# Moving the LayerNorm's normalisation from VectorE to ScalarE, and re-placing six small jobs, in a fused attention and mixture-of-experts kernel

## The chip, the cores and the metric

The kernel is one launch on one core of a Trainium2 chip. The metric is the device time in microseconds (us). The kernel before took 1573.0 us, the median of 3 runs (1572.06 to 1573.33).

## The reference, cut to what matters

The input is `x`, 64 sequences of 128 rows by 256, with a context of 64 x 128 x 192. Two layers follow one another.

```
x = x + attention(layernorm(x), context)   # 16 heads of 64; q = n @ Wq, k,v = ctx @ Wkv, softmax, @ Wproj + bproj
x = x + experts(layernorm(x))              # 8 experts 256x256, silu, top 2 of a softmax gate, then combine_w
layernorm(x) = (x - mean) / sqrt(var + 1e-5)
```

Everything is float32. The kernel keeps a product's precision by splitting each operand into a high part (`fp32r`) and a low part (what the high part leaves), and adding three products.

## The kernel before, in words

**Pairs and slots.** Two sequences make a pair; there are 32 pairs. The attention of a pair has 8 slots (`u` 0 to 7), one for each pair of heads. A slot is a row of instructions on each engine that `for s, i, u in slots()` writes out: slot `s`, pair `i`, number `u`. The slots before slot 0 (`i == -1`) are the start, those after pair 31 the tail. Each engine runs its own instructions strictly in the order in which they stand; semaphores hold an engine back until another has got far enough.

**What a slot holds.** TensorE (PE): `turn_probs` of the head pair before (4 transposes), `queries_keys` three head pairs ahead (11 matmuls), `scores` of the next head pair (6), then the slot's general jobs ("mid"), then `attend` (6) and `project` (6), and in late slots the `expert` and `combine` products. ScalarE (ACT): `exps`, `pT`, `attended`, `qk` and then the high parts of the general jobs. VectorE (DVE): `inverse` (the sums of the exponentials and their reciprocals), `pT`, `qk`, `row_max`, then the low parts of the general jobs. GpSimd (POOL): `split_attended`, `normalise_probs`, `scatter` and `gather` by indirect DMA, `rsqrt`, `split_ctx_lo`, `add_bias` in slot 0. So there is one chain for every slot: `turn_probs` (PE), `pT` and `attended` (ACT), `split_attended` and `normalise_probs` (POOL), and `turn_probs` of the next slot (PE).

**General jobs.** `ATTENTION_JOBS` says in which slot PE makes the values of the next pair (`value`, four jobs of 5 matmuls of 512 columns), the transposes of the two normalised inputs (`turn_x`, `turn_x1`), the gate and the ranks. They share three PSUM banks in turn.

**Experts.** Tokens are scattered to a sorted table, and 147 blocks of 128 sorted rows run through their experts, at one block a slot. The blocks are listed when a chunk of pairs is routed; the chunks end at pairs 8, 16, 22, 26 and 28. In the first slots after such a pair DVE runs `count_blocks`, `list_blocks` and `list_outputs`. Blocks fill the slots from pair 9 slot 6 to pair 14 slot 4, from 17.6 to 22.4, from 23.6 to 27.4, and from 27.6 to 32.3. The other slots, here called light, hold attention alone (and now and then a combine). The last four pairs' experts are computed densely, in the tail.

**LayerNorm.** For each of the two norms: DVE `norm_stats` and `norm_merge` (mean and variance, two of each), POOL `rsqrt` (`var_eps`, then `rstd` by a power), DVE `normalise` (two `tensor_scalar`, line 1006). For the next pair's `x` the statistics stand in slot 5 (of the pair two earlier), `rsqrt` in slot 6 and `normalise` in slot 1; for `x1` of the pair before they stand in slot 2, 2 and 3. `turn_x` is in slot 3, `turn_x1` in slot 4. `normalise(j, n)` waits for POOL's `rstd_done`, PE's `turn_x` and `turn_x1` wait for `xn_done` and `xn2_done`.

**The start.** SyncE (SP) loads the weights. ACT makes their high parts (`weight_hi`), DVE the low parts of the first six, POOL those of the rest of the keys (6 and 7) and of the projection. PE's `queries_keys(0, 2)`, in the last slot before slot 0, waits for all of these but the projection's. In slots 1 to 8 DVE prepares the expert weights (`expert_minus_last`) and POOL splits them. In pair 1 slot 0 SP writes zero rows into the sorted table (line 538).

Of the kernel before, what the change touches and what calls it, by code (L numbers as in the profile page):

```python
# [5 lines left out]
P = 128  # L6
# [37 lines left out]
    6: [("value", 1, 1)],  # L44
    7: [("rank", 0, -1)],
# [94 lines left out]
def xattn_moe_kernel(nc, x, ctxT, wq, wkv, wkv_rest, wproj, bproj, gateT, expertT, expert_b, combineT, out):  # L140
# [20 lines left out]
    with ExitStack() as stack:  # L161
# [93 lines left out]
        rstd = [sb(f"rstd{n}", [P, 2]) for n in (1, 2)]  # L255
        neg_max = [sb(f"neg_max{b}", [P, 4]) for b in range(2)]
# [83 lines left out]
        rstd_done = [sem(f"rstd_done{n}") for n in (1, 2)]  # L340

# [52 lines left out]
        FOR_FIRST, FOR_VALUES, BY_VECTOR, PROJECTION, EXPERTS_FROM, COMBINE_SPLIT = 3, 5, 6, 8, 9, len(SPLIT) - 1  # L394
        KEYS_BY_POOL = PROJECTION - BY_VECTOR
        PROJ_BY_POOL = KEYS_BY_POOL + 1
# [3 lines left out]
        def _(sp):  # L400
# [29 lines left out]
            def load_weights(n):  # L430

                if n >= EXPERTS_FROM:
                    sp.wait_ge(w_lo_dve, BY_VECTOR)
                if n > EXPERTS_FROM:
                    sp.wait_ge(w_lo_pool, KEYS_BY_POOL)
                of, to = WEIGHTS[n]
                sp.dma_start(to, of).then_inc(w_in[n], 16)
# [66 lines left out]
            for s, i, u in slots():  # L504
# [31 lines left out]
                if i == 1 and u == 0:  # L536
# [32 lines left out]
        def _(pe):  # L569
# [9 lines left out]
            def queries_keys(j, p):  # L579
# [7 lines left out]
                if j == 0 and p == 2:  # L587
                    pe.wait_ge(w_hi, PROJECTION)
                    pe.wait_ge(w_lo_dve, BY_VECTOR)
                    pe.wait_ge(w_lo_pool, KEYS_BY_POOL)  # L590
# [116 lines left out]
            def combine(m, bank):  # L707
                pe.wait_ge(drained["turn_mixed"], m + 1)
                if m == 0:
                    pe.wait_ge(w_lo_pool, COMBINE_SPLIT - BY_VECTOR + 1)  # L710
# [56 lines left out]
            pe.wait_ge(const_b, 2)  # L767
            for s, i, u in slots():
# [29 lines left out]
        def _(act):  # L798
# [6 lines left out]
            def weight_hi(n):  # L805
# [9 lines left out]
                act.activation(hi, raw, ACT.Copy, scale=QSCALE if n in (0, FOR_VALUES) else 1.0).then_inc(w_hi, 1)  # L815

# [93 lines left out]
            for s, i, u in slots():  # L910
# [46 lines left out]
        def _(dve):  # L957
# [6 lines left out]
            def weight_lo(n):  # L964
# [5 lines left out]
                else:  # L970
                    rows = HALF if n in (2, 4) else P
# [17 lines left out]
            def stats_ready(j, n):  # L989
                dve.wait_ge(bn_done[n], 2 * j + 2)  # L990
                wait(dve, (xn_done, xn2_done)[n], j)
# [10 lines left out]

            def normalise(j, n, src, to, done, width=C):
                dve.wait_ge(rstd_done[n], j + 1)
                for t in range(2):
                    last = dve.tensor_scalar(to[:, t, 0:width], src[:, t, 0:width], mv[n][:, t, 0:1], rstd[n][:, t:t + 1],
                                             ALU.subtract, ALU.mult)
                last.then_inc(done, 1)
# [161 lines left out]
            def count_blocks():  # L1170
# [5 lines left out]
                link(dve.tensor_tensor_scan(rows_to[:, :], rows_new[:, :], zeros[:, :], 0.0, ALU.add, ALU.add))  # L1176
                link(dve.tensor_tensor(rows_from[:, :], rows_to[:, :], rows_new[:, :], ALU.subtract))
# [60 lines left out]
            for s, i, u in slots():  # L1238
# [42 lines left out]
                if u == (1 if i > 0 else 2) and nxt:  # L1281
                    normalise(i + 1, 0, x_raw, x_raw, xn_done)
                if u == 3 and before:
                    wait(dve, made["turn_x1"], i - 1)
                    wait(dve, scattered[(i - 1) % 2], 64 * min((i - 1) // 2, (SPARSE + i % 2) // 2))
                    if i - 1 < 2:
                        dve.wait_ge(const_c, 3)
# [35 lines left out]
        def _(pool):  # L1323
# [14 lines left out]
            def rsqrt(j, n):  # L1338
                pool.wait_ge(mv_done[n], 2 * j + 2)
                wait(pool, rstd_done[n], j)  # L1340
# [139 lines left out]
```

## Time and profile before

| what | value |
|---|---|
| median of 3 runs | 1573.0 us |
| the profiled execution | 1573.3 us |
| its span, first to last instruction | 1571.6 us |
| mean granted TensorE clock, share of full speed | 0.994 |
| busy: PE, DVE, ACT, POOL | 95%, 82%, 67%, 59% |

The profiled execution's time is 1.7 us more than its span and 0.3 us over the median. Busy shares are averages over the span: a PE that is called busy may still run matmuls at a wider spacing than it can. L12 is line 12 of the kernel, `a<-b,c` what an instruction writes and reads, `x4` the number of instructions that one row merges. A wait is put down to what released it.

### The profile page before, as it was taken

How to read it: one execution, taken by the hardware profiler on the slowest of the kernel's cores; microseconds unless marked ns; L12 is line 12 of the kernel's file. 1: busy time of each engine (PE TensorE's matmuls, PEld its weight loads, DVE VectorE, ACT ScalarE, POOL GpSimd, SP SyncE). 2: the span in 40 equal slices, each digit the busy share in tenths (PEclk: the TensorE clock that was granted, in tenths of full speed). 3: DMA queues.
4: the chain of work that ended last, by engine and by line, in shares of the span. 5: the costliest groups of instructions: out<-in, count | busy, mean ns of one | idle time of the engine just before them, and what ended most of it. 6: DMA issues, size and time to landing. Idle time of an engine off the chain costs nothing.

```text
span 1571.6 us, 38337 instructions
## 1 busy us (share of the span) xinstructions
PE 1499.9 (95%) x11648; PEld 1435.2 (91%) x11648; DVE 1292.8 (82%) x3153; ACT 1057.0 (67%) x2891; POOL 923.7 (59%) x1215
## 2 busy tenths in 40 slices
PE   5999999999999999999999999999999999999796
PEld 4889999999899999999999999989999999999675
DVE  6988888888888888888888888888888888877566
ACT  4766776766667766676667677767777676767432
POOL 5756666666555655577666555576666466655510
PEclk9999999999999999999999999999999999999999
DMA  8543333333577777455677777568888777877822
GB/s 241 179 132 97 95 94 94 96 95 98 169 223 229 224 219 215 110 135 146 196 236 235 208 225 220 161 172 241 244 241 239 232 223 236 266 215 222 279 61 81
DMA packets 180474, 287.77 MB, mean 183 GB/s; under 512 B 23600, under 2 KB 115248, under 8 KB 180016
## 3 DMA queue, kind: packets, MB, share of 16 engines
q1 hardware_dynamic: 169520, 255.94, 57.2%
q0 software_dynamic: 10752, 29.37, 5.7%
q8 instruction: 97, 1.59, 0.4%
q14 instruction: 105, 0.86, 0.2%
HBM read 156.51 MB, written 61.60 MB: 139 GB/s over the span
## 4 chain that ended last, share of the span: by engine, by line
PE 75%; DVE 12%; issue 6%; ACT 4%; POOL 3%; DMA 1%; SPq 0%; ACTq 0%; DVEq 0%; POOLq 0%
PE gen_ps L572 20%; PE qk_ps L572 17%; PE o_ps L572 9%; PE proj_ps L572 9%; PE s_ps L572 9%; PE pT_ps L617 6%; PE gen_ps L695 2%; DVE neg_max L1019 1%; DVE sums L1026 1%; PE gen_ps L662 1%; PE gen_ps L670 1%; DVE pT_s_lo L961 1%; DMA k_s<-qk_s 1%; ACT v_s_hi L802 1%; ACT stage L802 1%
## 5 line engine op out<-in xcount | busy, mean ns | idle before, releaser
L1357 POOL CAST o_s_hi<-stage 128x256 fp32r<-128x256 f32 x256 | 102.0, 398 | 413.7 <-ACT stage L802 409.8
L828 ACT ACTIVATE stage<-s_ps,neg_max 128x128 f32<-128x128 f32 x1024 | 292.1, 371 | 73.9 <-DVE neg_max L1019 69.8
L1348 POOL TENSOR_TENSOR stage<-stage,inv_sums 128x512 f32<-128x512 f32 x256 | 265.9, 1039 | 10.2 <-DVE inv_sums L1028 10.1
L802 ACT CAST pT_s_hi<-pT_ps 128x512 fp32r<-128x512 f32 x256 | 150.6, 588 | 129.6 <-PE pT_ps L617 119.9
L572 PE MATMUL s_ps<-k_s,qk_s 128*128 128x256 f32 x1536 | 226.7, 284 | 3.6 <-DMA k_s<-qk_s 3.3
L1026 DVE TENSOR_REDUCE sums<-stage 128x4 f32<-128x512 f32 x256 | 172.7, 675 | 45.3 <-ACT stage L828 32.4
L961 DVE TENSOR_TENSOR qk_s<-qk_ps,qk_s 128x512 fp32r<-128x512 f32 x256 | 176.3, 689 | 39.2 <-ACT qk_s L802 34.4
L572 PEld LDWEIGHTS s_ps<-k_s,qk_s 128*128 128x128 f32 x1536 | 201.7, 189 | 4.4 <-DMA k_s<-qk_s 3.9
L1359 POOL TENSOR_TENSOR o_s_lo<-stage,o_s_hi 128x256 fp32r<-128x256 f32 x256 | 188.2, 735 | 20.9
L961 DVE TENSOR_TENSOR pT_s_lo<-pT_ps,pT_s_hi 128x512 fp32r<-128x512 f32 x256 | 171.9, 672 | 30.4 <-ACT pT_s_hi L802 24.2
L802 ACT CAST v_s_hi<-gen_ps 128x512 fp32r<-128x512 f32 x129 | 75.8, 587 | 178.0 <-PE gen_ps L572 176.1
L802 ACT COPY stage<-o_ps 64x256 f32<-64x256 f32 x512 | 188.0, 367 | 3.1
L572 PE MATMUL qk_ps<-xT_hi,wq_s_hi 128*128 128x256 f32 x512 | 165.6, 323 | 11.7 <-DVE cT_hi L1013 4.8
L1019 DVE TENSOR_REDUCE neg_max<-s_ps 128x4 f32<-128x512 f32 x256 | 174.4, 681 | 0.9 <-PE s_ps L572 0.9
L572 PE MATMUL o_ps<-pT_s_hi,v_s_hi 128*128 128x256 f32 x512 | 155.6, 304 | 16.5 <-DVE pT_s_lo L961 14.3
L802 ACT CAST qk_s<-qk_ps 128x512 fp32r<-128x512 f32 x256 | 149.7, 585 | 29.5 <-PE qk_ps L572 18.3
L617 PE MATMUL pT_ps<-ident,stage 128*128 128x128 f32 x1024 | 154.8, 273 | 1.4 <-POOL stage L1348 1.0
L572 PE MATMUL proj_ps<-wproj_s_hi,o_s_hi 128*128 128x256 f32 x512 | 146.6, 286 | 3.2 <-POOL o_s_lo L1359 2.8
L572 PE MATMUL qk_ps<-xT_hi,wq_s_lo 128*128 128x256 f32 x512 | 145.1, 283 | 0.0
L572 PE MATMUL o_ps<-pT_s_hi,v_s_lo 128*128 128x256 f32 x512 | 144.9, 283 | 0.0
L572 PE MATMUL o_ps<-pT_s_lo,v_s_hi 128*128 128x256 f32 x512 | 144.4, 282 | 0.0
L572 PE MATMUL qk_ps<-xT_lo,wq_s_hi 128*128 128x256 f32 x512 | 144.3, 282 | 0.0
(347 smaller groups left out, 4655.4 us busy)
## 6 DMA issues: line engine op xcount, KB each, us to landing
w_block<-expert_table SPq DMA_DIRECT2D x147, 512.0 KB
k_s<-qk_s SPq DMA_DIRECT2D x512, 128.0 KB
stage<-sorted_x SPq DMA_DIRECT2D x147, 128.0 KB
sorted_y<-stage SPq DMA_DIRECT2D x147, 128.0 KB
x_raw<-in_x SPq DMA_DIRECT2D x32, 256.0 KB
c_raw<-in_ctxT SPq DMA_DIRECT2D x32, 256.0 KB
stage<-in_x SPq DMA_DIRECT2D x32, 256.0 KB, 3.5
x_kept<-x SPq DMA_DIRECT2D x32, 256.0 KB
```

Of the source, the lines that this page charges most:

```text
L572: mm = pe.matmul(out_ap, l, r, start=start and n == 0, stop=stop and n == len(terms) - 1, skip_group_check=skip)
L617: mm = pe.transpose(pT_ps[:, k * P:(k + 1) * P], probs[p % 2][:, k, :], ident[:, :])
L662: mm = pe.matmul(bank[:, a * N2 + t * P:a * N2 + (t + 1) * P], src[:, 2 * t + k, a * P:(a + 1) * P], ident[:, :], is_transpose=True, start ...
L695: mm = pe.transpose(bank[:, a * P:(a + 1) * P], x_block[n % RING][:, a * P:(a + 1) * P], ident[:, :])
L802: last = act.copy(to, of)
L828: last = act.activation(probs[p % 2][:, k, :], s_ps[:, k * P:(k + 1) * P], ACT.Exp, bias=neg_max[p % 2][:, k:k + 1])
L961: last = dve.tensor_tensor(lo, of, hi.bitcast(F32), ALU.subtract)
L1019: dve.tensor_reduce(neg_max[p % 2][:, :], s_ps[:, :].rearrange("p (k n) -> p k n", k=4), AX_X, ALU.max, negate=True).then_inc(max_done, 1)
L1026: dve.tensor_reduce(sums[p % 2][:, :], probs[p % 2][:, :, :], AX_X, ALU.add).then_inc(sums_done, 1)
L1348: pool.tensor_tensor(probs[b][:, :, :], probs[b][:, :, :], inv_sums[b][:, :].unsqueeze(2).broadcast_to([P, 4, P]), ALU.mult).then_inc(prob ...
L1357: pool.tensor_copy(hi[:, :, :], o_full).then_inc(o_hi, 1)
L1359: pool.tensor_tensor(lo[:, :, :], o_full, hi[:, :, :].bitcast(F32), ALU.subtract).then_inc(o_lo, 1)
```

## The change

The diff, cut to its core. Left out are the new buffers and semaphores (`minus_rstd`, `minus_mean`, `minus_one`, `minus_done`, `shift_done`), a memset of `minus_one`, and the counts of `w_lo_dve` and `w_lo_pool` that follow from who makes which low part.

```diff
-    6: [("value", 1, 1)],
-    7: [("rank", 0, -1)],
+    7: [("rank", 0, -1), ("value", 1, 1)],
...
+        BY_POOL, LAST_KEYS, PROJECTION = 6, 7, 8
+        BY_VECTOR, PROJ_BY_POOL = 7, 2
...  SP, the zero rows
-                if i == 1 and u == 0:
+                if i == 4 and u == 0:
...  PE, before the slots, after const_b
+            for n in range(16):
+                pe.transpose(gen_ps[BANKS - 1][:, 0:P], ident[:, :], ident[:, :])
...  ACT
+            def normalise(j, n, src, to, done, width=C):
+                act.wait_ge(shift_done[n], j + 1)
+                for t in range(2):
+                    last = act.activation(to[:, t, 0:width], src[:, t, 0:width], ACT.Identity,
+                                          bias=minus_mean[n][:, t:t + 1], scale=rstd[n][:, t:t + 1])
+                last.then_inc(done, 1)
...  ACT, in the slots, after general(s, "mid")
+                if u == 2 and nxt:
+                    normalise(i + 1, 0, x_raw, x_raw, xn_done)
+                if u == 3 and before:
+                    wait(act, made["turn_x1"], i - 1)
+                    wait(act, scattered[(i - 1) % 2], 64 * min((i - 1) // 2, (SPARSE + i % 2) // 2))
...
+                    normalise(i - 1, 1, x1, xn2[(i - 1) % 2], xn2_done, C - 1)
...  DVE
-                    rows = HALF if n in (2, 4) else P
+                    rows = HALF if n in (2, 4, LAST_KEYS) else P
...
-            def normalise(j, n, src, to, done, width=C):
-                dve.wait_ge(rstd_done[n], j + 1)
...
+            def chunk_rows():
                 link(dve.tensor_tensor(rows_from[:, :], rows_to[:, :], rows_new[:, :], ALU.subtract))
                 link(dve.tensor_tensor(choices[:, 0, :], begun[:, :], rows_from[:, :], ALU.subtract))
...
-                if s in (-SLOTS, 0):
+                if u == 0 and nxt:
                     x_stats(i + 1)
-                if u == 5 and i >= 0 and exists(i + 2):
-                    x_stats(i + 2)
...
-                if u == (1 if i > 0 else 2) and nxt:
-                    normalise(i + 1, 0, x_raw, x_raw, xn_done)
-                if u == 3 and before:
...
-                    normalise(i - 1, 1, x1, xn2[(i - 1) % 2], xn2_done, C - 1)
...
                     if u == 0:
                         count_blocks()
                     if u == 1:
+                        chunk_rows()
+                    if u == 3:
                         list_blocks(plan.ends.index(i - 1))
...
+                if i == -1 and u == 6:
+                    weight_lo(LAST_KEYS)
...  POOL, in rsqrt, after rstd
+                pool.wait_ge(rstd_done[n], j + 1)
+                pool.tensor_tensor(minus_rstd[n][:, :], rstd[n][:, :], minus_one[:, :], ALU.mult).then_inc(minus_done[n], 1)
+                pool.wait_ge(minus_done[n], j + 1)
+                pool.tensor_tensor(minus_mean[n][:, :], mv[n][:, :, 0], minus_rstd[n][:, :], ALU.mult).then_inc(shift_done[n], 1)
...
-                if s in (-SLOTS + 1, 1):
+                if u == 1 and nxt:
                     rsqrt(i + 1, 0)
-                if u == 6 and i >= 0 and exists(i + 2):
-                    rsqrt(i + 2, 0)
...
-                    for n in range(BY_VECTOR, PROJECTION):
-                        weight_lo(n)
+                    weight_lo(BY_POOL)
```

So `x` is normalised as `rstd * x + minus_mean`, where `minus_mean` is the mean times minus `rstd`; `count_blocks` keeps its first five operations.

## Rows read from the trace of the kernel before

**Rows 1.** The page, part 1: busy us (share of the span) x instructions.

```profile
PE 1499.9 (95%) x11648; PEld 1435.2 (91%) x11648; DVE 1292.8 (82%) x3153; ACT 1057.0 (67%) x2891; POOL 923.7 (59%) x1215
```

**Rows 2.** Busy us (instructions) by stretch, clock, DMA share, GB/s.

```profile
100.00:200.00 100.00, 98.42 (x768) 94.25 (x768) 81.01 (x208) 69.72 (x193) 62.55 (x85) 1.00 0.36 89
500.00:600.00 100.00, 100.00 (x812) 97.95 (x811) 85.54 (x212) 69.92 (x199) 53.16 (x72) 1.00 0.78 224
```

**Rows 3.** Timeline of the start: start us, us, engine, line, [idle before <-releaser].

```profile
6.97 1.14 DVE L1006 TENSOR_SCALAR x_raw<-x_raw,mv,rstd 128x256 f32<-128x256 f32 x2 [1.11 <-POOL rstd L1343]
11.35 0.55 PE L572 MATMUL qk_ps<-xT_hi,wq_s_hi 128*128 128x256 f32 x1 [2.00 <-DVE xT_lo L961]
16.82 0.41 PE L572 MATMUL qk_ps<-xT_lo,wq_s_hi 128*128 128x256 f32 x1
17.19 0.28 PE L572 MATMUL qk_ps<-cT_hi,wkv_s_hi 128*128 128x256 f32 x1
18.21 1.76 DVE L968 SCALAR_TENSOR_TENSOR wq_s_lo<-stage,wq_s_hi 128x1536 fp32r<-128x1536 f32 x1 [0.70 <-ACT wq_s_hi L815]
19.00 2.65 POOL L1330 TENSOR_TENSOR wkv_s_lo<-stage,wkv_s_hi 128x768 fp32r<-128x768 f32 x1 [11.36 <-ACT wkv_s_hi L815]
21.60 1.80 POOL L1330 TENSOR_TENSOR wkvr_s_lo<-stage,wkvr_s_hi 128x768 fp32r<-128x768 f32 x1
23.66 0.36 PE L572 MATMUL qk_ps<-xT_hi,wq_s_hi 128*128 128x256 f32 x1 [4.54 <-POOL wkvr_s_lo L1330]
```

**Rows 4.** Timeline of pair 1, slots 0 to 2.

```profile
76.39 2.38 SPq L420 DMA_DIRECT2D k_s<-qk_s  x2
82.11 0.97 PE L572 MATMUL s_ps<-k_s,qk_s 128*128 128x256 f32 x6 [1.99 <-DMA k_s<-qk_s]
```

**Rows 5.** Timeline of pair 0, slots 2 and 3, and of slot 7.

```profile
42.16 1.73 DVE L1006 TENSOR_SCALAR x_raw<-x_raw,mv,rstd 128x256 f32<-128x256 f32 x2
46.28 0.38 PE L572 MATMUL o_ps<-pT_s_hi,v_s_hi 128*128 128x256 f32 x1 [1.06 <-DVE pT_s_lo L961]
...
66.85 0.39 PE L572 MATMUL o_ps<-pT_s_hi,v_s_hi 128*128 128x256 f32 x1 [0.71 <-DVE pT_s_lo L961]
```

**Rows 6.** Timeline of pair 5, a light pair: slots 3 and 4.

```profile
243.10 1.15 ACT L828 ACTIVATE stage<-s_ps,neg_max 128x128 f32<-128x128 f32 x4
243.80 0.60 PE L617 MATMUL pT_ps<-ident,stage 128*128 128x128 f32 x4
244.97 0.19 POOL L1341 TENSOR_TENSOR var_eps<-mv,eps 128x2 f32<-128x2 f32 x1 [0.85 <-DVE mv L995]
247.09 1.04 POOL L1348 TENSOR_TENSOR stage<-stage,inv_sums 128x512 f32<-128x512 f32 x1
247.74 1.14 ACT L828 ACTIVATE stage<-s_ps,neg_max 128x128 f32<-128x128 f32 x4 [0.20 <-DVE neg_max L1019]
248.18 0.66 PE L617 MATMUL pT_ps<-ident,stage 128*128 128x128 f32 x4
252.54 0.60 PE L617 MATMUL pT_ps<-ident,stage 128*128 128x128 f32 x4
```

**Rows 7.** Groups of instructions: busy us, mean ns | idle before.

```profile
L896 ACT ACTIVATE stage<-stage,top_w 128x256 f32<-128x256 f32 x112 | 47.7, 501 | 0.0
```

**Rows 8.** One line's instructions: duration ns min/median/max, first and last start.

```profile
L1103 DVE SCALAR_TENSOR_TENSOR top_w<-gate_exp,gate_inv x32: 161/164/1609, 115.6 to 1534.4; 128x4 f32<-128x4 f32 x32
L987 DVE BATCH_NORM_STATS2 stats<-x_raw x64: 407/414/421, 4.8 to 1352.3; 128x6 f32<-128x256 f32 x64
```

**Rows 9.** Timeline of slot 0: pair 5, then pair 9 with its block count.

```profile
234.48 0.69 DVE L1026 TENSOR_REDUCE sums<-stage 128x4 f32<-128x512 f32 x1 [0.89 <-ACT stage L828]
234.85 1.31 POOL L1366 TENSOR_TENSOR stage<-stage,bias_row 128x512 f32<-128x512 f32 x1
...
391.38 2.14 DVE L1175 TENSOR_TENSOR rows_new<-rounded,begun 128x9 f32<-128x9 f32 x1
392.17 1.31 POOL L1366 TENSOR_TENSOR stage<-stage,bias_row 128x512 f32<-128x512 f32 x1
```

More of the change, by code:

```diff
@@ L255, in xattn_moe_kernel @@
         rstd = [sb(f"rstd{n}", [P, 2]) for n in (1, 2)]
+        minus_rstd = [sb(f"minus_rstd{n}", [P, 2]) for n in (1, 2)]
+        minus_mean = [sb(f"minus_mean{n}", [P, 2]) for n in (1, 2)]
+        minus_one = sb("minus_one", [P, 2])
         neg_max = [sb(f"neg_max{b}", [P, 4]) for b in range(2)]
@@ L340, in xattn_moe_kernel @@
         rstd_done = [sem(f"rstd_done{n}") for n in (1, 2)]
+        minus_done = [sem(f"minus_done{n}") for n in (1, 2)]
+        shift_done = [sem(f"shift_done{n}") for n in (1, 2)]
         dense_tanh, dense_added, dense_w_done = (sem(n) for n in ("dense_tanh", "dense_added", "dense_w_done"))
@@ L392, in xattn_moe_kernel @@
         SPLIT.append((stage[:, 2, 0:2 * C], *[w[:, :, :].rearrange("p a n -> p (a n)") for w in wcomb_s]))
-        FOR_FIRST, FOR_VALUES, BY_VECTOR, PROJECTION, EXPERTS_FROM, COMBINE_SPLIT = 3, 5, 6, 8, 9, len(SPLIT) - 1
-        KEYS_BY_POOL = PROJECTION - BY_VECTOR
-        PROJ_BY_POOL = KEYS_BY_POOL + 1
+        FOR_FIRST, FOR_VALUES, EXPERTS_FROM, COMBINE_SPLIT = 3, 5, 9, len(SPLIT) - 1
+        BY_POOL, LAST_KEYS, PROJECTION = 6, 7, 8
+        BY_VECTOR, PROJ_BY_POOL = 7, 2
         QSCALE = float(HALF) ** -0.5
@@ L434, in load_weights @@
                 if n > EXPERTS_FROM:
-                    sp.wait_ge(w_lo_pool, KEYS_BY_POOL)
+                    sp.wait_ge(w_lo_pool, 1)
                 of, to = WEIGHTS[n]
@@ L589, in queries_keys @@
                     pe.wait_ge(w_lo_dve, BY_VECTOR)
-                    pe.wait_ge(w_lo_pool, KEYS_BY_POOL)
+                    pe.wait_ge(w_lo_pool, 1)
                 wait(pe, qk_lo, j * HEAD_PAIRS + p)
@@ L709, in combine @@
                 if m == 0:
-                    pe.wait_ge(w_lo_pool, COMBINE_SPLIT - BY_VECTOR + 1)
+                    pe.wait_ge(w_lo_pool, PROJ_BY_POOL + E + 1)
                 for t in range(2):
@@ L938, in _ @@
                 general(s, "mid")
+                if u == 2 and nxt:
[3 more added lines that the diff above has]
+                    wait(act, scattered[(i - 1) % 2], 64 * min((i - 1) // 2, (SPARSE + i % 2) // 2))
+                    if i - 1 < 2:
+                        act.wait_ge(const_c, 3)
+                    normalise(i - 1, 1, x1, xn2[(i - 1) % 2], xn2_done, C - 1)
                 if s in plan.mix and plan.pair_of[plan.mix[s]] < SPARSE:
@@ L990, in stats_ready @@
                 dve.wait_ge(bn_done[n], 2 * j + 2)
-                wait(dve, (xn_done, xn2_done)[n], j)
+                wait(dve, shift_done[n], j)
             def norm_merge(n):
@@ L1001, in x_stats @@
                 norm_merge(0)
-            def normalise(j, n, src, to, done, width=C):
-                dve.wait_ge(rstd_done[n], j + 1)
[L1005 to L1008, printed above, removed]
             def rest_lo(j):
@@ L1280, in _ @@
                     norm_merge(1)
-                if u == (1 if i > 0 else 2) and nxt:
-                    normalise(i + 1, 0, x_raw, x_raw, xn_done)
-                if u == 3 and before:
[L1284 to L1287, printed above, removed]
-                    normalise(i - 1, 1, x1, xn2[(i - 1) % 2], xn2_done, C - 1)
                 if u == 4 and nxt:
@@ L1339, in rsqrt @@
                 pool.wait_ge(mv_done[n], 2 * j + 2)
-                wait(pool, rstd_done[n], j)
+                wait(pool, (xn_done, xn2_done)[n], j)
                 pool.tensor_tensor(var_eps[n][:, :], mv[n][:, :, 1], eps[:, :], ALU.add).then_inc(eps_done[n], 1)
@@ L1400, in _ @@
             pool.memset(eps[:, :], EPS)
+            pool.memset(minus_one[:, :], -1.0)
             pool.memset(minus_half[:, :], -0.5).then_inc(zeroed, 2)
```

## The prediction

> **What bounds the kernel.** I read the page first: PE is busy for 1499.9 of 1571.6 us [rows 1], so at most 72 us are idle, and no job leaves PE but for the order. Then the windows: where expert blocks run, PE is busy for 100.00 of 100 us with 812 matmuls; in light stretches it runs 768 and DVE only 81 [rows 2]. So between expert blocks nothing can be gained, little can be lost, and the change is decided in the start, in pairs 0 and 1 and in the light slots. The timelines of these places came next, with one question at each wait of PE: who is late.
>
> In the start PE waits until 11.35 for the first low part, and then from its last value product (started at about 18.7) to 23.66 for the low part of the last keys, which POOL makes in 2.65 and 1.80 us one after the other [rows 3]. In pair 1 it waits 1.99 us for the spread keys [rows 4], in pair 0 1.06 us for DVE, which had normalised x for 1.73 us just before, and 0.71 us at the end of pair 0, where DVE has no idle time [rows 5]. In light pairs the reader is to look at the distance between the `turn_probs` of two slots: 243.80, 248.18, 252.54, that is 4.38 and 4.36 us [rows 6], while PE's own work there is some 3.9 us. `turn_probs` at 248.18 starts when POOL's `normalise_probs` (247.09, 1.04 us) ends. The chain of a slot (PE's transposes, ACT's `pT` and `attended`, POOL's split and multiply) sets the pace there, and DVE's normalisation at slot 3 isn't in it.
>
> **Part by part.** The price of ACT's normalisation: the trace has no Identity with two pointer operands; the nearest row is ACT's scaled copy of the same 128x256, 47.7 us for 112, so 0.43 us each, 0.85 us for two [rows 7]. From below the 64-row copies of `attended` would give 0.74 for two; from above the 0.50 us of one alone gives 1.0. I take 0.85. POOL's two added operations on 128x2 are like `var_eps`, 0.19 us each [rows 6], and with their waits 0.5 us a norm.
>
> *The start.* POOL's addition (0.5) and the change of engine make the normalised x late by 0.2 us only, since two normalisations took 1.14 us on DVE [rows 3]. But on ACT it stands before the high parts of the context and the first weights, which were made while DVE worked: they slip by 0.85 us, and the first product from 11.35 to 12.2. All to the last high part slips by as much. Then DVE makes the last part in half the rows beside POOL. POOL ends part 6 at 19.00 + 0.85 + 2.65 = 22.5; DVE's part 7 is half of POOL's rows, under 1 us on DVE, after its 1.76 us part at 18.21 + 0.85 and the keys of slot -2, so at 22.5 too. `queries_keys(0, 2)` starts at 22.6 for 23.66: -1.05. The value job that filled the wait (5 products, 1.2 us) now stands after the first scores; PE has time there, but ACT makes its high part before the first exponentials: +0.7. Together -0.4. Between -2 (ACT's queue hidden) and +1 (nothing of the split gained).
>
> The 16 early transposes end before x is ready and cost nothing. Their possible gain: products started every 0.21 us at 16.82 and every 0.12 us after 17.19 (durations 0.41 and 0.28) [rows 3]; were the clock up at 12.2, about 2.1 us of the 24 products before POOL's part would go. No row shows transposes alone raising the clock: four ran at 8.26 and the clock rose 8.8 us later. I take 0. The Trainium skill, "TensorE: Matmul & The Clock Gate", Part 4, says that transposes do not count as busy for the clock gate; by it the gain is 0 as well, by the row alone it stays open.
>
> *Pairs 0 and 1.* The write of zero rows leaves the stretch in which keys of pair 1 landed 3.3 us after their issue ended; in pair 4 the same keys have some 6 us: -2.0, the whole wait [rows 4]. DVE is rid of 1.73 us in pair 0 slot 2, but the exponentials follow ACT's 0.85 us there: -0.7 of the 1.06. Statistics leave slot 5 of pair 0: -0.7 of the late wait [rows 5], given back by half when they stand in slot 0 of pair 1 before DVE's expert rows: net -0.3. POOL's longer `rsqrt` before the combine weights: +0.5. Light slots 3 and 4 of pair 1 (below): +0.8. Sum -1.7, between -4 and +1.
>
> *Light pairs.* Slot 2: exponentials started at 243.10 directly after the value's high part; now 0.85 us later. `pT` and `attended` follow by 0.5 us later than before (0.24 to 0.3 us were idle). POOL's `rsqrt` at 244.97 gets 0.5 us longer and stands before the same split, so the two delays coincide: `normalise_probs` ends at 248.6 for 248.13, +0.5. Slot 3: ACT runs exponentials, `pT`, `attended`, keys, context, x and now x1: 4.9 us, in a slot of 4.4. The exponentials of 247.74 (0.20 us idle before) come 1.3 later, `attended` about 0.7 to 0.9 later, and `turn_probs` at 252.54 by 0.9 in sum [rows 6]. Slot 5 holds the gate and a value job; it is PE's own and gives nothing back.
>
> Slot 0 adds 0.2: the statistics, 0.41 us each and never longer, now stand before DVE's weights of the gate, an operation of 0.16 to 1.61 us [rows 8]. The long ones are those that meet POOL's add of the bias. At 391.38 another small DVE operation with two inputs ran 2.14 us and ended when POOL's 1.31 us add had [rows 9]. In pair 5 it would now begin at 234.35 and end with the add, at 236.2, for sums that started at 234.48: late by 1.6, of which 1.4 are slack. The Trainium skill, "Advanced Engine Details and Errata", GPSIMD Details, states that POOL shares an interface with VectorE's instructions of two SBUF inputs; the trace agrees (2.14 us), and by the rule the 0.2 stands.
>
> Slots 6 and 7: PE waited 0.3 us in slot 7 for DVE; with the value job there it doesn't, but slot 6 without it becomes light and is set by the chain, 4.3 us: -0.1. And -0.05 at the gate's slot. Per light pair 0.9 + 0.2 - 0.15 = 0.95; the terms overlap in ACT's queue, so I take 0.8. Light in slots 3 and 4 are pairs 2 to 9, 15 and 23 (16 and 17 have a combine in slot 3 that covers it): 10 x 0.8 = +8. From below -0.3 a pair (the removed wait alone, the rest hidden), from above 1.3.
>
> *Chunk ends.* Five times `count_blocks` meets the bias add (2.14 us of wait in one [rows 9]). The statistics before it fill that time, and two operations of 0.2 us leave: -0.4 each, -2.0. `list_blocks` in slot 3 meets other POOL work: +0.2 each, +1.0. Sum -1.0, from -5 to +4. SP needs the list at slot 4, after the last scatter of slot 3 anyway.
>
> *Blocks and tail.* With 1.7 us more PE work a slot, ACT's 0.85 fits: 0, at most +0.3 for each of 16 pairs. Tail: one norm, 0 (within 1).
>
> Sum on the profiled 1573.3: -0.4 - 1.7 + 8 - 1.0 = +4.9, 1578.2. I set 1577.5, since of the slack at each link I have counted only what shows as idle time. The median shown is 0.3 lower.
>
> **Rivals.** (a) ACT's additions hide in light slots: the exponentials have a whole slot until their `turn_probs`, ACT is busy 70 of 100 us [rows 2], and if POOL's queue regains 0.5 us in each slot, only the removed waits remain. Then 1573.3 - 0.4 - 1.7 - 1 - 0.1 x 10 - 0.8 (pair 1) = 1568.4, faster. It decides from a light-slot loss below 0.3 us a pair. Against it: idle of 0.20 us only before the exponentials of slot 3 [rows 6]. (b) The transposes raise the clock: 2.1 us off the forecast, 1575.4; with (a), 1566. (c) The loss reaches the block slots too, 16 x 0.3 = 5 more: 1582.5; against it the 100% of PE there.
>
> **Chances.** Forecast 0.45, (a) 0.27, (b) with the forecast's slots 0.15, (c) 0.13. A change under 0.2% (3.1 us) can't be told from none. Slower (above 1576.1): 0.38 of the forecast, 0.06 of (b), (c): 0.57, less some for a sum that is all small terms: 0.5. Same: 0.24. Faster: 0.26. Range 1567 to 1584; the forecast's own is 1574.5 to 1580.5.
>
> **What would show it.** Right: in pair 5 the `turn_probs` of slots 3, 4 and 5 lie 4.9 and 4.7 us apart where they were 4.4; a light pair takes 40.1 us instead of 39.3; no wait for keys in pair 1; first keys of head pair 2 at 22.6; the gate weights' median duration at 1.6 us in light pairs. Wrong: light slots of 4.4 us as before, or a granted clock already up at the first product.

## The result, and the profile after

The kernel after takes 1586.8 us (median of six, 1585.5 to 1588.3) where the kernel before took 1574.2 on the same chip: a ratio of 1.0075, 95% interval 1.0062 to 1.0088, so some 12 us slower. (One of the six executions of the kernel before took 8273 us; with it left out, the median is 1573.3.) The same kernel measured again beside other kernels, as after_again, gave 1.0101 (1.0075 to 1.0126). I had forecast 1577.5, and 1584 as the upper end: the direction is right, the size nearly three times too small.

The profiled execution took 1585.64 us with a span of 1583.9, against 1573.3 and 1571.6. Part 1 of its page answers to [rows 1]:

```profile
PE 1519.9 (96%) x11664; PEld 1441.8 (91%) x11664; DVE 1254.6 (79%) x3026; ACT 1112.8 (70%) x3019; POOL 949.3 (60%) x1343
```

DVE lost 38 us of work, ACT took on 56 and POOL 26. The windows answer to [rows 2]; the third is the stretch from the last scores to the end:

```profile
100.00:200.00 100.00, 98.69 (x748) 91.66 (x748) 80.79 (x195) 71.26 (x197) 62.19 (x90) 1.00 0.37 95
500.00:600.00 100.00, 100.00 (x815) 98.19 (x814) 83.52 (x201) 76.59 (x215) 58.73 (x87) 1.00 0.77 226
1461.60:1583.90 122.30, 93.25 (x499) 79.09 (x497) 76.03 (x171) 46.62 (x106) 29.58 (x37) 0.91 0.42 142
```

PE has 748 matmuls in 100 us of light slots where it had 768, and as many as before (815 for 812) where expert blocks run. The loss is in the light slots. The same last stretch of the kernel before:

```profile
1451.80:1571.60 119.80, 90.32 (x499) 76.31 (x497) 76.39 (x173) 45.61 (x104) 29.14 (x35) 0.94 0.43 143
```

It holds the same 499 matmuls in 2.5 us less, at a granted clock of 0.94 for 0.91. So in this profile the last scores came 9.8 us later than before, and the other 2.5 us are clock in the tail. That split varies from one execution to another: in after_again, a second profile of the same kernel with the same span, the last scores came 13.8 us later and the tail took 118.2 us at 0.94.

The start, answering to [rows 3], and then the keys of pair 1 [rows 4] (`SPq` is SyncE's DMA queue):

```profile
7.54 1.09 ACT L828 ACTIVATE x_raw<-x_raw,minus_mean,rstd 128x256 f32<-128x256 f32 x2 [1.95 <-POOL minus_mean L1360]
12.43 0.55 PE L576 MATMUL qk_ps<-xT_hi,wq_s_hi 128*128 128x256 f32 x1 [2.62 <-DVE cT_hi L1029]
19.64 2.65 POOL L1343 TENSOR_TENSOR wkv_s_lo<-stage,wkv_s_hi 128x768 fp32r<-128x768 f32 x1 [9.70 <-ACT wkv_s_hi L822]
21.42 1.69 DVE L995 TENSOR_TENSOR wkvr_s_lo<-stage,wkvr_s_hi 64x768 fp32r<-64x768 f32 x1
23.21 0.55 PE L576 MATMUL qk_ps<-xT_hi,wq_s_hi 128*128 128x256 f32 x1 [5.08 <-DVE wkvr_s_lo L995]
...
76.24 1.20 SPq L424 DMA_DIRECT2D k_s<-qk_s  x2
80.76 0.88 PE L576 MATMUL s_ps<-k_s,qk_s 128*128 128x256 f32 x6
```

The keys of head pair 2 come at 23.21 for 23.66, and in pair 1 PE doesn't wait for spread keys any more. VectorE's low part in half the rows takes 1.69 us: it ends 0.82 us after POOL's part 6 (`wkv_s_lo`), beside which it started (in start_only it takes 1.09 us and again ends 0.82 us after POOL's). Slots 3 to 5 of pair 5, the light pair of [rows 6]:

```profile
246.00 1.09 ACT L828 ACTIVATE x_raw<-x_raw,minus_mean,rstd 128x256 f32<-128x256 f32 x2
246.70 0.60 PE L621 MATMUL pT_ps<-ident,stage 128*128 128x128 f32 x4
247.00 1.12 ACT L843 ACTIVATE stage<-s_ps,neg_max 128x128 f32<-128x128 f32 x4
249.20 0.20 POOL L1360 TENSOR_TENSOR minus_mean<-mv,minus_rstd 128x2 f32<-128x2 f32 x1
250.52 1.03 POOL L1365 TENSOR_TENSOR stage<-stage,inv_sums 128x512 f32<-128x512 f32 x1
250.73 1.10 ACT L828 ACTIVATE xn<-x,minus_mean,rstd 128x255 f32<-128x255 f32 x2
251.60 0.66 PE L621 MATMUL pT_ps<-ident,stage 128*128 128x128 f32 x4
251.72 1.13 ACT L843 ACTIVATE stage<-s_ps,neg_max 128x128 f32<-128x128 f32 x4
256.28 0.66 PE L621 MATMUL pT_ps<-ident,stage 128*128 128x128 f32 x4
```

ACT's normalisation stands directly ahead of the exponentials in both slots. The `turn_probs` lie 4.90 and 4.68 us apart, for 4.38 and 4.36. Slot 0, answering to [rows 9], first in pair 5, then in pair 9, where a chunk ends:

```profile
236.31 1.04 POOL L1397 DMA_INDIRECT sorted_x<-xn,row_of  x1 [0.16 <-issue]
236.90 1.80 DVE L1119 SCALAR_TENSOR_TENSOR top_w<-gate_exp,gate_inv 128x4 f32<-128x4 f32 x1
237.37 1.30 POOL L1383 TENSOR_TENSOR stage<-stage,bias_row 128x512 f32<-128x512 f32 x1
238.63 0.67 DVE L1042 TENSOR_REDUCE sums<-stage 128x4 f32<-128x512 f32 x1
...
398.20 1.98 DVE L1188 TENSOR_SCALAR rounded<-filled 128x9 f32<-128x9 f32 x1
398.84 1.30 POOL L1383 TENSOR_TENSOR stage<-stage,bias_row 128x512 f32<-128x512 f32 x1
403.40 0.39 PE L576 MATMUL o_ps<-pT_s_hi,v_s_hi 128*128 128x256 f32 x1 [1.87 <-DVE pT_s_lo L984]
```

An operation on 128x4 takes 1.80 us, one on 128x9 1.98 us: each starts during the issue of POOL's scatter, which stands directly ahead of the add of the bias, and ends only when that add has (after_bias, below, shows that it is the add and not the scatter that holds them). Behind them wait the sums. Over all pairs (the lines' instructions, ns min/median/max, as [rows 8]):

```profile
L1119 DVE SCALAR_TENSOR_TENSOR top_w<-gate_exp,gate_inv x32: 161/1264/2046, 115.5 to 1545.6; 128x4 f32<-128x4 f32 x32
L828 ACT ACTIVATE x_raw<-x_raw,minus_mean,rstd x64: 585/596/605, 7.5 to 1393.4; 128x256 f32<-128x256 f32 x64
```

### The profile page after: what moved, and what is told of

Same layout as the page of the kernel before. It is cut to its first block, busy times and chain, and to the rows that moved or that the text cites. A ratio compares the mean times of both kernels' runs of the same rounds, so it can differ in the third digit from the quotient of the medians.

```text
span 1583.9 us, 38497 instructions
## 1 busy us (share of the span) xinstructions
PE 1519.9 (96%) x11664; PEld 1441.8 (91%) x11664; DVE 1254.6 (79%) x3026; ACT 1112.8 (70%) x3019; POOL 949.3 (60%) x1343
## 4 chain that ended last, share of the span: by engine, by line
PE 76%; DVE 9%; ACT 7%; issue 6%; POOL 1%; DMA 0%; ACTq 0%; DVEq 0%; SPq 0%; POOLq 0%
PE gen_ps L576 20%; PE qk_ps L576 17%; PE o_ps L576 10%; PE s_ps L576 9%; PE proj_ps L576 9%; PE pT_ps L621 6%; PE gen_ps L699 2%; PE gen_ps L666 1%; PE gen_ps L674 1%; ACT qk_s L809 1%; ACT stage L843 1%; DVE neg_max L1035 1%; ACT pT_s_hi L809 1%; DVE sums L1042 1%; DVE pT_s_lo L984 1%
## 5 line engine op out<-in xcount | busy, mean ns | idle before, releaser
L576 PE MATMUL o_ps<-pT_s_hi,v_s_hi 128*128 128x256 f32 x512 | 154.4, 302 | 12.9 <-DVE pT_s_lo L984 10.2
L576 PE MATMUL proj_ps<-wproj_s_hi,o_s_hi 128*128 128x256 f32 x512 | 149.9, 293 | 2.5 <-POOL o_s_lo L1376 2.3
```

Of the source, the lines that this page charges most:

```text
L576: mm = pe.matmul(out_ap, l, r, start=start and n == 0, stop=stop and n == len(terms) - 1, skip_group_check=skip)
```

## The experiments

In the table, "light pair" is the time from the first scores of pair 5 to those of pair 6 in the profile, and "last scores" how much later than in the kernel before (profiled at 1451.85 us) the last ones started. The second is free of the tail, but takes in any fall of the clock ahead of it. "Ratio" is to the kernel before on the same chip; medians of different rows can come from different chips, so the kernels are compared by it.

| kernel | median us | ratio, 95% | light pair | last scores |
|---|---|---|---|---|
| after | 1586.8 | 1.0075 (1.0062 to 1.0088) | 40.37 | +9.8 |
| after_again | 1588.4 | 1.0101 (1.0075 to 1.0126) | 40.37 | +13.8 |
| dve_norm | 1581.8 | 1.0047 (1.0029 to 1.0065) | 39.81 | +9.7 |
| x1_dve | 1583.5 | 1.0052 (1.0035 to 1.0070) | 40.06 | +13.0 |
| weights_first | 1585.3 | 1.0066 (1.0043 to 1.0088) | 40.07 | +9.3 |
| before_act | 1596.3 | 1.0136 (1.0112 to 1.0159) | 39.91 | +22.1 |
| pool_ops | 1585.8 | 1.0078 (1.0049 to 1.0107) | 40.20 | +13.3 |
| no_shift | 1584.9 | 1.0090 (1.0060 to 1.0120) | 40.38 | +10.2 |
| stats_back | 1573.4 | 1.0008 (0.9991 to 1.0025) | 39.23 | -1.9 |
| start_only | 1567.2 | 0.9981 (0.9964 to 0.9999) | 39.23 | -7.1 |
| bridge | 1568.5 | 0.9977 (0.9958 to 0.9995) | 39.29 | -5.5 |
| after_bias | 1574.2 | 1.0007 (0.9993 to 1.0022) | 40.06 | -1.1 |
| bias_early | 1565.5 | 0.9945 (0.9924 to 0.9967) | 39.23 | -10.8 |
| ends_only | 1562.4 | 0.9931 (0.9909 to 0.9953) | 39.25 | -13.2 |

The kernel before has 39.26. Not in the table: shift_dve (1.0624) and shift_early (1.0106), told below.

**dve_norm: the normalisations back on VectorE.**

```diff
-                    last = act.activation(to[:, t, 0:width], src[:, t, 0:width], ACT.Identity,
-                                          bias=minus_mean[n][:, t:t + 1], scale=rstd[n][:, t:t + 1])
+                    last = dve.tensor_scalar(to[:, t, 0:width], src[:, t, 0:width], mv[n][:, t, 0:1],
+                                             rstd[n][:, t:t + 1], ALU.subtract, ALU.mult)
```

> The kernel after, with both normalisations back on VectorE in slots 2 and 3 and POOL's two added operations a norm taken out; all else stays. Theory (the ScalarE normalisations lengthen the light slots' chain): slots 3 to 5 of a light pair go back by 0.84 us in sum, the slot-1 wait of 0.32 us stays, since the statistics stand in slot 0 all the same, so a light pair takes 39.5 us for 40.4 and the kernel 1573 to 1577 us. Rival 1 (the moved statistics and the value job in slot 7 cost it, not the engine of the normalisation): a light pair stays at 40.2 us or above and the time at 1584 or above. Rival 2 (the clock in the tail costs 2.6 us by itself): the tail after the last scores stays 2.6 us longer than in the kernel before.

A light pair fell by 0.56 us only, to 39.81, and the time by 0.3%, where I expected some 10 us. Half of what light pairs lose is not ScalarE's. And behind three of the five chunk ends the kernel lost more than after did (1.3, 0.6 and 1.3 us in pairs 9, 17 and 23): VectorE has the tokens and the block list in one slot,

```profile
409.00 1.14 DVE L1013 TENSOR_SCALAR xn<-x,mv,rstd 128x255 f32<-128x255 f32 x2
410.07 0.70 DVE L1192 TENSOR_SCALAR inside<-rows_to,block_row 128x9 f32<-128x9 f32 x1
412.04 0.67 DVE L1033 TENSOR_REDUCE sums<-stage 128x4 f32<-128x512 f32 x1
413.56 0.39 PE L576 MATMUL o_ps<-pT_s_hi,v_s_hi 128*128 128x256 f32 x1 [1.64 <-DVE pT_s_lo L968]
```

and PE waits 1.64 us where after waits 0.33. With the tokens on ScalarE the list costs little there, which I hadn't counted for it. That, and two stretches at a granted clock of 0.50 in this profile, 1.5 us each (pairs 17 and 23, slot 2), are why its last scores come as late as those of after.

**x1_dve: the tokens alone back on VectorE** (x stays on ScalarE; `normalise(i - 1, 1, ...)` of slot 3 moves, POOL's two operations for it go).

> The kernel after, with the tokens' normalisation alone (slot 3) back on VectorE and POOL's two added operations of this norm taken out; x stays on ScalarE in slot 2. Theory (slot 3 is where ScalarE's queue was full, the step that costs 0.53 of the 0.84 us): a light pair loses 0.55 to 0.75 us less, 39.7 us, and the kernel takes 1578 to 1580 us. Rival (both normalisations cost alike, 0.42 each, in proportion to their ScalarE time): 39.95 us a light pair, 1581 to 1582 us. Second rival (POOL's longer combine of statistics in slot 2 before the split is what delays the chain, and both theories read ScalarE wrongly): most of 0.84 goes, as the norm of the tokens is the one whose operations POOL has in slot 2.

A light pair took 40.06 us: 0.31 less, nearer to the first rival than to the theory, and below both. All of it is slot 5; slot 4 took as long as with both on ScalarE.

**weights_first: the gate's weights ahead of the statistics in slot 0.**

```diff
+                if u == 0 and exists(i - 2):
+                    route_weights(i - 2)
                 if u == 0 and nxt:
                     x_stats(i + 1)
```

> The kernel after, with VectorE's weights of the gate put ahead of the statistics of x in slot 0 instead of behind them. Theory (the gate weights now meet POOL's add of the bias and end only with it, so that the sums, the reciprocal and attended of slot 1 come late): the wait of PE in slot 1 of a light pair goes, 0.32 us less in each of some 11 to 13 pairs, 1583 us. Rival (it is the statistics' own 1.6 us of VectorE time that delay the sums, in whichever order): no change, 1586 to 1587 us. A second rival: the statistics themselves then meet the add, and the loss moves on to them.

The theory holds: 0.30 us less a light pair; the add came only after the statistics, so the second rival didn't get its test. The whole (1.0066 for 1.0075) can't be told from after: slot 2 got 0.2 to 0.4 us longer in five later pairs, where blocks run, and 0.7 us in pairs 27 and 29.

**before_act: the kernel before, with ScalarE's normalisations alone.**

> The kernel before, with the ScalarE normalisations alone (x in slot 1 for all but the first two blocks of rows, the tokens in slot 3) and POOL's two operations a norm; the statistics stay in slots 5 and 6, the value job in slot 6, the start as before. Theory: the loss of a light pair comes mostly with the engine of the normalisation, so this kernel has 0.6 to 0.9 us more a light pair, 40.0 us for 39.3, and takes 1580 to 1584 us. Rival (the loss needs x and the tokens in neighbouring slots 2 and 3; with x in slot 1 it spreads and hides): 0.3 us or less a light pair, 1574 to 1577 us. Nothing changes in the start, so no -1.9 us of the keys' wait in pair 1.

The light pair is as expected (39.91, +0.65), the time isn't: +22 us. Some 13 of them arise in pairs 16 to 19 and 24 to 30, which have combines and blocks; pair 24, slot 0:

```profile
1078.10 0.39 PE L577 MATMUL proj_ps<-wproj_s_hi,o_s_hi 128*128 128x256 f32 x1 [1.09 <-POOL o_s_lo L1369]
```

Here POOL's added operations stand ahead of gathers and splits in slot 6, and ScalarE's in slot 1. Which of the two it is wasn't tried. In after, with both at other places, pair 24 has no such wait.

**pool_ops and no_shift: POOL's part and ScalarE's part by themselves.** pool_ops is dve_norm with POOL's two operations kept:

```diff
+                pool.wait_ge(rstd_done[n], j + 1)
+                pool.tensor_tensor(minus_rstd[n][:, :], rstd[n][:, :], minus_one[:, :], ALU.mult).then_inc(minus_done[n], 1)
+                pool.wait_ge(minus_done[n], j + 1)
+                pool.tensor_tensor(minus_mean[n][:, :], mv[n][:, :, 0], minus_rstd[n][:, :], ALU.mult).then_inc(shift_done[n], 1)
```

> As dve_norm (both normalisations on VectorE), but POOL keeps its two added operations a norm, which nothing reads. The kernel after lost 0.62 us more a light pair than dve_norm did (0.31 us each at the scores of slots 4 and 5). Theory 1 (it is ScalarE's 0.85 us a norm in a queue with no room): the added POOL operations alone cost nothing, a light pair stays at 39.8 us. Theory 2 (it is POOL's 0.5 us in slot 2, in front of the split of attended that the projection waits for): 0.3 us or more of the 0.62 come back here, in slot 3, so 40.1 us or above.

no_shift is after without these four lines and with a bias of zero, which leaves the mean in x and in the tokens; ScalarE waits for `rstd` instead.

> The kernel after with POOL's two added operations left out and a bias of zero in ScalarE's normalisation, which leaves the mean in x and in the tokens; the work of every other instruction is the same. Theory (ScalarE and POOL lie side by side, the longer sets the slot): scores 4 to 5 of a light pair take 4.9 us (4.96 in after, 4.66 with the normalisations on VectorE), 5 to 6 stay at 5.16, a light pair 40.3 us. Rival (POOL's operations are the whole loss of slot 4): 4.66 us there, and 40.05 us a light pair. The end of the kernel 1583 to 1587 us by the first, 1582 to 1584 by the second.

The `turn_probs` of slots 3, 4 and 5 of pair 5, in dve_norm, in pool_ops and in no_shift:

```profile
242.91 0.60 PE L621 MATMUL pT_ps<-ident,stage 128*128 128x128 f32 x4
247.59 0.60 PE L621 MATMUL pT_ps<-ident,stage 128*128 128x128 f32 x4
251.91 0.60 PE L621 MATMUL pT_ps<-ident,stage 128*128 128x128 f32 x4
```

```profile
246.08 0.60 PE L621 MATMUL pT_ps<-ident,stage 128*128 128x128 f32 x4
251.11 0.66 PE L621 MATMUL pT_ps<-ident,stage 128*128 128x128 f32 x4
255.49 0.60 PE L621 MATMUL pT_ps<-ident,stage 128*128 128x128 f32 x4
```

```profile
246.49 0.60 PE L621 MATMUL pT_ps<-ident,stage 128*128 128x128 f32 x4
251.35 0.65 PE L621 MATMUL pT_ps<-ident,stage 128*128 128x128 f32 x4
256.08 0.66 PE L621 MATMUL pT_ps<-ident,stage 128*128 128x128 f32 x4
```

The two distances are 4.68 and 4.32 with neither, 5.03 and 4.38 with POOL's operations, 4.86 and 4.73 with ScalarE's, and 4.90 and 4.68 with both. So each alone costs 0.4 and 0.57 us a light pair, and both together 0.56: they lie side by side. To take away POOL's saves nothing (40.38 for 40.37), to take away ScalarE's 0.17 us (40.20). These are the slots' times in the profiles; by their ratios the kernels with either or both (1.0075 to 1.0101) can't be told apart.

**shift_dve and shift_early** were my first tries at the same question: VectorE makes the shift in one operation, in slots 2 and 3 behind the statistics, or at the slots' start.

```diff
+                dve.scalar_tensor_tensor(out=minus_mean[n][:, :], in0=mv[n][:, :, 0], scalar=-1.0, in1=rstd[n][:, :],
+                                         op0=ALU.mult, op1=ALU.mult).then_inc(shift_done[n], 1)
```

> The kernel after (both normalisations on ScalarE), with the shift, minus mean times rstd, made by VectorE in one operation in slots 2 and 3, in place of POOL's two. With pool_ops this completes the square: slot 4 (scores 4 to 5) of a light pair took 4.66 us with neither, 5.09 with POOL's operations alone, 4.96 with both. Theory (the two delays lie side by side and the longer sets the slot, ScalarE's being 0.26): slot 4 is 4.92 us, slot 5 stays 5.16, a light pair 40.3 us, so that POOL's operations aren't what can be saved: 1585 to 1587 us. Rival (POOL's queue is what sets slot 4): slot 4 falls by 0.3 us, a light pair to 40.0, 1582 to 1584 us.

> As shift_dve, with VectorE's one operation for the shift at the start of slots 2 and 3, where rstd was made a slot earlier, so that nobody waits for it. ScalarE normalises, POOL has no added operation. Theory (ScalarE's delay and POOL's lie side by side, the longer sets the slot): slot 4 (scores 4 to 5) of a light pair 4.9 us, slot 5 5.16, slot 2 still 5.39, a light pair 40.3, some 1585 to 1587 us. Rival (POOL's operations are the loss and ScalarE's part hides once they are gone): slot 4 at 4.66, a light pair 40.05 or less, 1582 to 1584 us.

Both missed. In shift_dve (1671.9 us) ScalarE waited for VectorE at the end of slot 2 with the next exponentials behind it, in shift_early (1587.7 us) VectorE waited for POOL's `rstd` with the sums behind it:

```profile
260.95 1.09 ACT L828 ACTIVATE x_raw<-x_raw,minus_mean,rstd 128x256 f32<-128x256 f32 x2 [1.75 <-DVE minus_mean L1029]
```

```profile
250.18 0.16 DVE L1029 SCALAR_TENSOR_TENSOR minus_mean<-mv,rstd 128x2 f32<-128x2 f32 x1 [1.11 <-POOL rstd L1366]
250.26 0.69 DVE L1048 TENSOR_REDUCE sums<-stage 128x4 f32<-128x512 f32 x1
```

An operation of 0.16 us cost 3.1 us a light pair in the first: what it waits for is its price.

**stats_back: dve_norm with the statistics in slots 5 and 6 and x in slot 1, as before.**

```diff
-                if u == 0 and nxt:
-                    x_stats(i + 1)
+                if u == 5 and i >= 0 and exists(i + 2):
+                    x_stats(i + 2)
-                if u == 2 and nxt:
+                if u == (1 if i > 0 else 2) and nxt:
                     normalise(i + 1, 0, x_raw, x_raw, xn_done)
```

> As dve_norm, and the statistics of x are back in slots 5 and 6 and its normalisation in slot 1, as before the change. What is left of the change is the start, the value job in slot 7 and the block list split and moved to slot 3. Theory: of the 0.54 us that dve_norm still lost a light pair, 0.32 go with the gate weights behind the statistics, and 0.23 with the normalisation of x in slot 2 instead of 1, so here a light pair takes 39.2 us, as before or 0.05 less, and the light pairs lose nothing. At the ends of chunks the block list in slot 3 stands with VectorE's normalisation of the tokens: 1.3 us each as in dve_norm, in at least 3 of 5. Together with the start's -1.7 that is 1573 to 1576 us. Rival: the value job in slot 7 is dearer than its 0.05 us gain once the statistics share slot 5 with the gate: 39.4 us or more.

39.23 us a light pair, 1573.4 us: the theory holds. From dve_norm to here is 0.4% of the time, from after to dve_norm 0.3%; with some 0.2% of uncertainty in each, the places of the statistics and of x cost as much as ScalarE's and POOL's operations.

**start_only and bridge: the kernel before with the edits of the start.** bridge has ten more transposes between those of x and the first product:

```diff
+                if j == 0 and p == 0:
+                    for n in range(10):
+                        pe.transpose(pT_ps[:, 0:P], ident[:, :], ident[:, :])
```

> The kernel before with the change's edits of the start alone: low part of the last keys on VectorE in half the rows, the 16 early transposes, the write of zero rows in pair 4. Theory: the wait for spread keys in pair 1 goes (1.9 us), the keys' low part gives up to 1 us, the rest is untouched: 2 to 3 us less than before, 1571 to 1572 us. Rival (the transposes raise the clock before the first product in some executions, and it then falls again in the gap before it, later than it would rise otherwise): the start loses some 1 us, and the sum is 1 us less than before or nothing.

> As start_only, with ten more transposes of the identity between those of x and the first product, so that TensorE has no idle time of 2 us there. Theory (in the other runs products of 256 columns came 0.214 us apart until 16.2 to 18.3 us and 0.119 us after; the gap before the first product is what keeps the clock low): the products come 0.12 us apart from the first on, so that up to 2.4 us of the first 24 products go, of which the wait for POOL's low part at 22 us takes back all but 0 to 0.5: 1570.5 to 1572 us. Rival (transposes don't raise it; only the products do): products 0.214 us apart until 15.9 or later, and the time of start_only within 0.3 us.

start_only is faster than the kernel before, by 0.19% (0.01 to 0.36). In its profile 4.8 us are gained by pair 2, but that differs from one execution to another: kernels with this start and VectorE's normalisation gained 2.0 to 4.8 us there. In bridge the products came 0.12 us apart from the second on:

```profile
9.08 1.68 PE L582 MATMUL pT_ps<-ident 128*128 128x128 f32 x10
11.35 0.35 PE L572 MATMUL qk_ps<-xT_hi,wq_s_hi 128*128 128x256 f32 x1 [0.59 <-issue]
11.54 0.28 PE L572 MATMUL qk_ps<-xT_lo,wq_s_hi 128*128 128x256 f32 x1
```

But the time stayed: 1568.5 for 1567.2, which can't be told apart. PE only waits longer for the low parts at 22 us, as expected.

**after_bias, bias_early, ends_only: POOL's add of the bias moved from slot 0 to slot 7 of the pair before**, in after, in start_only, and in start_only for the five last pairs of chunks alone.

```diff
-                if u == 0 and before:
-                    add_bias(i - 1)
+                if u == 7 and now:
+                    add_bias(i)
```

> The kernel after, with POOL's add of the bias moved from slot 0 to slot 7 of the pair before. Theory (the gate weights of slot 0 and, at the ends of chunks, the count of blocks end only with that add): the 0.32 us of slot 2 go in some 12 light pairs (3.8 us), and of the five waits of 0.8 to 2.07 us at the ends of chunks more than half goes (4 to 8 us): 1575 to 1579 us, and a light pair takes 40.05 us. Rival (the add meets other operations of VectorE in slot 7 just as well): slot 7 or slot 0 gets 0.3 us or more longer and the time falls by less than 4 us.

> As start_only (the kernel before with the change's edits of the start), with POOL's add of the bias moved from slot 0 to slot 7 of the pair before. Theory: the five waits in slot 2 at the ends of chunks (1.91, 2.17, 1.89, 1.28 and 1.24 us), in which the count of blocks waited for the add, lose together 4 to 7 us; light pairs stay at 39.2: 1561 to 1564 us, or a ratio of 0.993 to 0.995 to before, and less spread, since the clock doesn't fall behind those waits. Rival (count and list of blocks are some 2.5 us of VectorE's own time in a slot of 4.3 and that is the wait): less than 2 us in sum, 1566 us or more.

> As start_only, with POOL's add of the bias moved to slot 7 only for the five last pairs of chunks (8, 16, 22, 26 and 28), whose add stood beside the count of blocks. Theory: the waits at the five ends go as in bias_early (2.0, 1.1, 2.0, 1.3 and 1.4 us), and its losses in pairs 0 and 1 (2.7 us) don't come: some 7 to 8 us less than start_only, 1558 to 1562 us, ratio 0.990 to 0.992. Rival (the losses of bias_early in pairs 0 and 1 were the phase of the clock or the first DMAs, not the moved add): the same 7 to 8 us against its own start, but a start that differs by as much, 1562 to 1566 us.

> The kernel after once more, unchanged, so that the three others of this group stand beside it on one chip. All theories: ratio 1.0075 as measured, 12 us above before; a light pair 40.37 us, the last scores 9.8 us later than in before. Whatever of the span is not in these 9.8 us is stretches at half the granted clock behind the last scores, and differs from run to run by 1.7 us a stretch.

after_again has the light pair that was expected, but its last scores came 13.8 us later and not 9.8: two stretches at half the granted clock ahead of them, in pairs 9 and 23, make 3.1 us, and the start with pair 0 took 1.8 us longer.

In after the one move is worth as much as the change had lost (1574.2 us, 1.0007), but most of it isn't the same loss: of the 10.9 us by which its last scores come earlier, 8.1 are at the five chunk ends, where the kernel before waited too, and some 3 are the 0.3 us in slot 2 of the light pairs, which the change had added. Pair 9, slots 7 and 0, of after_bias:

```profile
390.87 1.29 POOL L1383 TENSOR_TENSOR stage<-stage,bias_row 128x512 f32<-128x512 f32 x1
396.33 1.03 POOL L1397 DMA_INDIRECT sorted_x<-xn,row_of  x1
396.75 0.14 DVE L1188 TENSOR_SCALAR rounded<-filled 128x9 f32<-128x9 f32 x1
398.19 0.16 DVE L1119 SCALAR_TENSOR_TENSOR top_w<-gate_exp,gate_inv 128x4 f32<-128x4 f32 x1
399.91 0.28 PE L576 MATMUL o_ps<-pT_s_hi,v_s_hi 128*128 128x256 f32 x1
```

The 1.98 us of L1188 are 0.14, though it starts during the same scatter's issue, and PE doesn't wait. The same operations of VectorE cost their own time when POOL's add isn't beside them; so the rival of bias_early (they fill the slot themselves) is out. In start_only PE's five waits at chunk ends are 7.7 us in sum (1.75, 2.01, 1.73, 1.13, 1.08), in ends_only two are left of 0.2 each. ends_only beats both kernels: 1562.4 us, 0.69% below the kernel before (0.47 to 0.91). bias_early lost 1.1 us each in slot 1 of pairs 16 and 17 and some in pairs 0 and 1; ends_only keeps the one in pair 17 (1.15 us). Its start was later than that of start_only by 1.5 us all the same, so what the moved add costs in pairs 0 and 1 stays open: first products come at 10.85 to 11.88 us in kernels with one start.

## Why the prediction was wrong, point by point

**Start and pairs 0 and 1: right as far as two profiles tell.** Forecast -2.1 up to pair 2, measured -1.7, and +0.1 in after_again. The wait of pair 1 went in both, and the pair took 1.9 us less. The first product came at 12.43 (forecast 12.2), the keys at 23.21 (22.6): VectorE's part wasn't done in under 1 us, it took 1.69 and ended behind POOL's part 6, so the split gained 0.45 us and not 1.05. With VectorE's normalisation the same edits gained 2.0 to 4.8 us up to pair 2.

**Slots 3 to 5 of light pairs: right in size, half right in cause.** I had 4.9 and 4.7 us, it was 4.90 and 4.68. But two terms were off and met: ScalarE's operation is 0.60 us, two take 1.09, for the 0.43 and 0.85 that I took from a copy of a scaled tile [rows 7]; and POOL's 0.5 us, which I said coincides, would by itself have cost 0.4. Also, with both normalisations on VectorE slot 4 took 4.68 us in dve_norm and 4.39 in stats_back, so 0.29 us come with the new places of x and its statistics; which of the two places it is wasn't tried, nor whether the 0.29 are there beside ScalarE's and POOL's parts (before_act, with x and its statistics at the old places, has 5.05).

**Slot 0: too small.** The gate weights end with POOL's add, as said; it costs 0.32 us a light pair, for 0.2 (in light pairs they take 1.80 us, for 1.6; the median over all pairs is 1.26). The Trainium skill, "Advanced Engine Details and Errata", GPSIMD Details, states that POOL shares an SBUF interface with VectorE's instructions of two SBUF inputs, as this one is; the trace agrees (1.80 us). The price is after_bias's: with the bias add elsewhere the kernel is 0.7% faster, chunk ends included.

**The step that failed is the sum over light pairs.** A light pair was worked out at 0.95 and then taken as 0.8, since "the terms overlap in ACT's queue": it is 1.11 (0.32 + 0.53 + 0.31 - 0.05). And the list of ten was short. By the first scores of each pair, pairs 2 to 9, 15 and 23 lost 10.2 us where I had 8 and -0.4 for their chunk ends; pairs 16 and 17, "covered" by a combine, lost 1.1 and 0.5, and pairs 14 and 22 0.5 each. These last two aren't ScalarE's: stats_back, with VectorE's normalisation in the old places, has the same 0.5, and start_only nothing, so they come with the value job in slot 7, for which I had no loss. That is 2.6 + 2.6 us of the 8 between 1577.5 and the profile's 1585.6; the tail has 2.5, and 0.7 I had taken off the sum of 1578.2 myself.

**Chunk ends: right as a sum, by luck.** -1.0 forecast: -0.4 for each wait and +0.2 for each list. The five waits went from 8.1 us (1.73, 2.11, 1.73, 1.30, 1.27) to 7.0 (1.87, 1.91, 1.87, 0.68, 0.68): three changed by 0.2 or less, two got 0.6 shorter. In slot 3 the list left a new wait of 0.33 us in pairs 9 and 23.

**Blocks: right**, 0.05 to 0.17 us a pair in most; but pairs 10, 18, 24 and 27 to 29 got 0.3 to 0.9 us shorter each, which I hadn't forecast. **Tail: 0 forecast, +2.5 in the profile**, which is clock and not work, as the windows show; after_again had 118.2 us there, 1.6 less than before.

**The rivals.** (a), that ScalarE's additions hide, is out: ScalarE's part alone costs 0.57 us a light pair (no_shift against dve_norm). (b), that the transposes raise the clock, happens in some executions, and where bridge made it last into the products, the time (1568.5 for 1567.2) couldn't be told from start_only's. (c), a loss in block slots, didn't come; its 1582.5 would have been nearer for the wrong reason.

**Where the 12 us come from.** By ratios, each with some 0.2% of uncertainty: the edits of the start -0.2%, value job and block list +0.3% (start_only to stats_back), statistics and x in their new slots +0.4% (to dve_norm), ScalarE's and POOL's operations +0.3% (to after; by after_again it would be 0.5%). The part that gives the change its name is a third to a half of it; in a light pair it is 0.56 of 1.11 us.

## What to carry to other kernels

Price a moved operation by what runs on the neighbouring engine at its new place: a VectorE operation of 0.14 us took 1.98 when it stood beside a 1.3 us add on POOL, and to move that add was worth more than any other edit here. When two engines in a chain each get longer, undo both at once to see the price; one alone shows little (0 and 0.17 of 0.56 us here). And a loss worked out per slot is to be counted over every slot that has it, and not rounded down for slack that no row shows.

## What the hardware showed that was not expected

**Transposes alone can raise the clock.** 16 transposes of the identity ran from 4.35; in weights_first and x1_dve the four of x at 8.7 took 0.66 us, in after 1.12, about as in the kernel before (1.09), which has no early ones. In the first two the clock then fell again: the products from 12.43 on were 0.21 us apart, and the granted clock of x1_dve reads 0.50 from 12.45 to 15.0. The Trainium skill, "TensorE: Matmul & The Clock Gate", Part 4, says that transposes do not count as busy for the gate; bridge, where only transposes ran between 4.32 and 10.8 and the second product came 0.19 us after the first and the third 0.11 after that, speaks against it.

**Behind waits of about 2 us the clock fell to half in some executions.** In after_again PE waited 1.88 us before 405.36, and the granted clock then reads 0.50 (the lower level, 1.2 GHz) at full work:

```profile
405.36 0.39 PE L576 MATMUL o_ps<-pT_s_hi,v_s_hi 128*128 128x256 f32 x1 [1.88 <-DVE pT_s_lo L984]
```

```profile
406.50:409.70 3.20, 3.20 (x17) 3.20 (x17) 2.39 (x8) 2.35 (x7) 1.86 (x6) 0.50 0.60 165
```

17 matmuls in 3.2 us, where the same profile has 26 in 3.3 us at a granted clock of 1.00 shortly before. That pair took 1.5 us more than in the first profile of after, with the same wait. Such stretches in the middle, ahead of the tail, came in six of fourteen profiles with these waits, twelve in all, eleven of them behind a wait of 1.75 to 2.02 us at a chunk end and one (before_act) behind a wait of 2.27 us for spread keys; they came in none of the three with the add moved. Three profiles are few, so that the waits cause them is likely and not shown.
